# Convolution as three short filters over even and odd blocks, in place of four, in a two-layer convolution and feed-forward kernel

## The reference

```python
def _layer(x, style, w, b, mw, mb, typ):
    s = style @ mw.T + mb
    weight = SCALE * w * s[:, None, :, None]
    demod = lax.rsqrt(jnp.sum(weight * weight, axis=(2, 3)) + EPS)
    weight = weight * demod[:, :, None, None]
...
out = x
for i, typ in enumerate(('same', 'upsample', 'same', 'downsample')):
    out = _layer(out, style, weights[i], biases[i], mod_w[i], mod_b[i], typ)
```

## Time and profile before

| | |
|---|---|
| median of 3 runs | 1592.81 us (1592.79 to 1595.31) |
| the profiled execution, its own time | 1594.2 us |
| its span, first to last instruction | 1592.3 us |
| PE / PEld busy | 1559.0 / 1376.3 us |
| DVE / ACT / POOL busy | 798.6 / 577.3 / 206.4 us |
| mean granted clock of TensorE | 0.995 |
| one pair in the steady state, layer 0 / layer 1 | about 22.5 us / 23.5 us |

### The profile page before, as it was taken

How to read it: one execution, slowest core, us unless ns; L and a number is a source line. 1 busy time by engine, 2 the same in 40 slices (tenths; PEclk the granted TensorE clock), 3 DMA queues, 4 the chain that set the end, 5 groups by cost and what they waited for, 6 DMA issues and landing times.

```text
span 1592.3 us, 25445 instructions
## 1 busy us (share of the span) xinstructions
PE 1559.0 (98%) x8503; PEld 1376.3 (86%) x8503; DVE 798.6 (50%) x2061; ACT 577.3 (36%) x1291; POOL 206.4 (13%) x280
## 2 busy tenths in 40 slices
PE   5999999999999999999999999999999999999998
PEld 4688888888888888888868999999999999999998
DVE  7645655454444444454555554454555455445443
ACT  3323442334333333333333333333334333333332
POOL 1101010111011101111100110111111011011010
PEclk9999998999999999999999999999999999999999
DMA  4352332332333233333262333332332333333331
GB/s 103 99 117 82 106 80 64 95 101 83 102 83 105 81 104 79 105 92 92 66 185 67 79 96 88 79 105 79 83 101 79 99 85 89 96 79 99 86 79 66
DMA packets 54331, 145.66 MB, mean 91 GB/s; under 512 B 17233, under 2 KB 19345, under 8 KB 54306
## 3 DMA queue, kind: packets, MB, share of 16 engines
q1 hardware_dynamic: 53616, 144.96, 33.4%
q10 hardware_dynamic: 690, 0.37, 0.1%
HBM read 111.75 MB, written 33.55 MB: 91 GB/s over the span
## 4 chain that ended last, share of the span: by engine, by line
PE 93%; DVE 3%; issue 2%; DMA 1%; ACT 1%; POOL 0%; SPq 0%; DVEq 0%; POOLq 0%
PE bank L1099 29%; PE bank L1101 29%; PE bank L1100 28%; PE bank L1364 4%; PE bank L1246 1%; DMA xraw<-x_dram 1%; PE bank L1310 0%; PE bank L1281 0%; DVE fw_l L884 0%; DMA win<-in_L_cond_weights_dram 0%; PE bank L1176 0%; PE bank L1178 0%; PE bank L1300 0%; PE bank L1370 0%; DVE win L907 0%
## 5 line engine op out<-in xcount | busy, mean ns | idle before, releaser
L1099 PE MATMUL bank<-fw_h,ct_h 128*128 128x512 f32 (+2 forms) x1280 | 458.9, 358 | 0.6 <-DVE xout L856 0.5
L1100 PE MATMUL bank<-fw_l,ct_h 128*128 128x512 f32 (+2 forms) x1280 | 450.3, 352 | 0.0
L1101 PE MATMUL bank<-fw_h,ct_l 128*128 128x512 f32 (+2 forms) x1280 | 449.3, 351 | 0.0
L348 POOL TENSOR_TENSOR x_l<-xraw,x_h 128x512 fp32r<-128x512 f32 x128 | 165.8, 1317 | 1258.1 <-ACT x_h L488 1258.1
L992 DVE TENSOR_TENSOR ct_l<-bank,ct_h 128x384 fp32r<-128x384 f32 (+1 forms) x256 | 96.2, 417 | 390.3 <-ACT ct_h L536 389.8
L1101 PEld LDWEIGHTS bank<-fw_h,ct_l 128*128 128x128 f32 x1280 | 241.0, 188 | 22.7
L1099 PEld LDWEIGHTS bank<-fw_h,ct_h 128*128 128x128 f32 x1280 | 241.2, 188 | 20.8 <-issue 1.0
L1100 PEld LDWEIGHTS bank<-fw_l,ct_h 128*128 128x128 f32 x1280 | 241.6, 189 | 16.4
L1099 PE MATMUL bank<-x_h,tw 128*128 128x512 f32 x640 | 253.1, 395 | 0.5 <-DVE tw L977 0.5
L1101 PE MATMUL bank<-x_h,tw 128*128 128x512 f32 x640 | 252.8, 395 | 0.0
L1100 PE MATMUL bank<-x_l,tw 128*128 128x512 f32 x640 | 251.8, 394 | 0.0
(11 more groups left out here) (203 smaller groups left out, 1783.1 us busy)
## 6 DMA issues: line engine op xcount, KB each, us to landing
xraw<-in_x_dram SPq DMA_DIRECT2D x32, 512.0 KB, 5.0
xres<-in_x_dram SPq DMA_DIRECT2D x32, 512.0 KB, 3.9
x_dram<-xout SPq DMA_DIRECT2D x32, 512.0 KB, 2.9
xraw<-x_dram SPq DMA_DIRECT2D x32, 512.0 KB, 5.0
xres<-x_dram SPq DMA_DIRECT2D x32, 512.0 KB, 3.9
out_dram<-xout SPq DMA_DIRECT2D x32, 512.0 KB, 2.9
xraw<-in_x_dram SPq DMA_DIRECT2D x32, 511.5 KB, 6.5
xraw<-x_dram SPq DMA_DIRECT2D x32, 511.5 KB, 6.5
```

The costliest lines, as they stand in the source:

```text
L348: nc.gpsimd.tensor_tensor(x_l[h][:, PAD:PAD + HL], src, x_h[h][:, PAD:PAD + HL].bitcast(F32), ALU.subtract).then_inc(s["x_ready"], 1)
L1099: mm(out, wh, xh, start=start, stop=False, skip_group_check=True)
L1100: mm(out, wh, xl, start=False, stop=False, skip_group_check=True)
L1101: return mm(out, wl, xh, start=False, stop=stop, skip_group_check=True)
```

## The change

With the filter taps t0 to t4 and the columns of the image split into even and odd blocks, the change computes one product P of the odd columns with sums of neighbouring taps (three filter blocks), and two products of differences of neighbouring columns with the taps: even taps t0, t2, t4 (three blocks) and odd taps t1, t3 (two blocks). The even outputs are P plus the first, the odd outputs P minus the second. That is 8 filter blocks of 256 columns per image where 5 of 512 stood.

- POOL makes the differences (`neighbours`), two operations of 128x512 per pair, and takes the low parts of differences and odd columns (four operations). It starts on the input of pair j+1 only after `t_ready` and `t_side` of both images of pair j (`x_next`).
- ACT rounds odd columns and differences of pair j+1 after the convolution of pair j (`x_high`), copies the whole filter tile of 8 blocks (`t_high`) and takes over the copy across partitions of the second kind (`t_side`, two operations per image). It scales P (`sum_scaled`, 254 columns) where it scaled the whole result.
- DVE scales the 5 blocks into `t_f`, adds neighbours into 3 more, subtracts the high part (8 blocks), and copies 8 blocks across partitions; after each convolution it makes odd and even outputs (`conv_out`, two operations of 254 columns). `w2_low` and `prep` now come between `conv_out(j, 0)` and `conv_out(j, 1)`.
- P goes to `comp_ps[h]`, the two others to the halves of `conv_ps[h]`.

```diff
...
+                def neighbours(j):
+
+                    pool.wait_ge(s["x_load"], 32 * j + 32)
+                    for h in range(2):
+                        m0, m1 = (xraw[:, h, at:at + L].rearrange("p (n e q) -> p e n q", e=2, q=2)[:, :, :, 0] for at in (0, 2))
+                        nc.gpsimd.tensor_tensor(d_f[h][:, :, :], m0, m1, ALU.subtract).then_inc(s["d_made"], 1)
+
+                def split_low(j):
+                    for h in range(2):
+                        pool.wait_ge(s["x_hi"], 2 * j + h + 1)
+                        nc.gpsimd.tensor_tensor(d_l[h][:, :, 1:QL + 1], d_f[h][:, :, :], d_h[h][:, :, 1:QL + 1].bitcast(F32),
+                                                ALU.subtract)
+                        nc.gpsimd.tensor_tensor(o_l[h][:, 1:QL + 1], xraw[:, h, 2:L:4], o_h[h][:, 1:QL + 1].bitcast(F32),
+                                                ALU.subtract).then_inc(s["x_ready"], 1)
...
+                def x_next(j):
+
+                    pool.wait_ge(s["t_ready"], 2 * j + 2)
+                    pool.wait_ge(s["t_side"], 2 * j + 2)
+                    neighbours(j + 1)
+                    split_low(j + 1)
+
+                def body(j, last=False):
+
+                    pool.wait_ge(s["t_ready"], 2 * j + 2)
+                    edges(j)
+                    if not last:
+                        x_next(j)
...
+                def x_high(j, h, first=False):
+
                     if not first:
-                        act.wait_ge(s["conv_acc"], 2 * j)
-                    for h in range(2):
-                        nc.scalar.copy(x_h[h][:, PAD:PAD + HL],
-                                       xraw[:, h, :].rearrange("p (m q) -> p m q", q=2)[:, :, 0]).then_inc(s["x_hi"], 1)
+                        act.wait_ge(s["conv_acc"], 2 * j + h - 1)
+                    act.wait_ge(s["d_made"], 2 * j + h + 1)
+                    nc.scalar.copy(o_h[h][:, 1:QL + 1], xraw[:, h, 2:L:4])
+                    nc.scalar.copy(d_h[h][:, :, 1:QL + 1], d_f[h][:, :, :]).then_inc(s["x_hi"], 1)
...
                 def t_high(j):
                     for h in range(2):
-                        act.wait_ge(s["t_acc"], 2 * j + h + 1)
-                        nc.scalar.activation(tw[h][:, 0, :, 0, :], comp_ps[h][:, 0:NSH * C].rearrange("p (u c) -> p u c", c=C),
-                                             ACT.Copy, scale=s_all[:, 0, bass.ds(2 * j + h, 1)]).then_inc(s["t_hi"], 1)
+                        act.wait_ge(s["g_made"], 4 * j + 2 * h + 2)
+                        nc.scalar.copy(tw[h][:, 0, :, 0, :], t_f[h][:, :, :]).then_inc(s["t_hi"], 1)
+                    for h in range(2):
+
+                        act.wait_ge(s["t_lo"], 2 * j + h + 1)
+                        nc.scalar.copy(tw[h][half(0), :, 1:NSH, 1, :], tw[h][half(1), :, 0:NSH - 1, 0, :].bitcast(F32))
+                        nc.scalar.copy(tw[h][half(0), :, G0:SLOTS:G1 - G0, 1, :],
+                                       tw[h][half(1), :, 0:GM + 1:GM, 0, :].bitcast(F32)).then_inc(s["t_side"], 1)
...
-                def conv_scaled(j, h):
-                    act.wait_ge(s["conv_acc"], 2 * j + h + 1)
-                    nc.scalar.activation(conv[h][:, 2:HL - 2], conv_ps[h][:, 2:HL - 2], ACT.Identity,
+                def sum_scaled(j, h):
+
+                    act.wait_ge(s["p_acc"], 2 * j + h + 1)
+                    nc.scalar.activation(conv[h][:, 2:HL - 2:2], comp_ps[h][:, 1:QL - 1], ACT.Identity,
                                          scale=lam4[:, bass.ds(2 * j + h, 1)],
...
-                    conv_scaled(j, 0)
+                    sum_scaled(j, 0)
+                    if not composed:
+                        w2_high(ly, j + 1)
+                    if not last:
+                        x_high(j + 1, 0)
                     if step is not None:
                         prep(step)
-                    conv_scaled(j, 1)
+                    sum_scaled(j, 1)
+                    if not last:
+                        x_high(j + 1, 1)
...
                 def t_low(j):
                     for h in range(2):
+
+                        full = t_f[h]
+                        dve.wait_ge(s["t_acc"], 2 * j + h + 1)
+                        v.tensor_scalar(full[:, 0:NSH, :], comp_ps[h][:, 0:NSH * C].rearrange("p (u c) -> p u c", c=C),
+                                        s_all[:, 0, bass.ds(2 * j + h, 1)], None, ALU.mult).then_inc(s["g_made"], 1)
+                        dve.wait_ge(s["g_made"], 4 * j + 2 * h + 1)
+                        v.tensor_tensor(full[:, G0:SLOTS, :], full[:, 0:3, :], full[:, 1:4, :], ALU.add).then_inc(s["g_made"], 1)
+                    for h in range(2):
                         dve.wait_ge(s["t_hi"], 2 * j + h + 1)
-                        low(tw[h][:, 1, :, 0, :], comp_ps[h][:, 0:NSH * C].rearrange("p (u c) -> p u c", c=C),
-                            s_all[:, 0, bass.ds(2 * j + h, 1)], tw[h][:, 0, :, 0, :]).then_inc(s["t_lo"], 1)
+                        v.tensor_tensor(tw[h][:, 1, :, 0, :], t_f[h][:, :, :], tw[h][:, 0, :, 0, :].bitcast(F32),
+                                        ALU.subtract).then_inc(s["t_lo"], 1)
 
                         dve.wait_ge(s["t_lo"], 2 * j + h + 1)
-                        v.tensor_copy(tw[h][half(1), :, :, 1, :], tw[h][half(0), :, :, 0, :].bitcast(F32))
-                        v.tensor_copy(tw[h][half(0), :, 1:NSH, 1, :], tw[h][half(1), :, 0:NSH - 1, 0, :].bitcast(F32)
-                                      ).then_inc(s["t_ready"], 1)
+                        v.tensor_copy(tw[h][half(1), :, :, 1, :], tw[h][half(0), :, :, 0, :].bitcast(F32)).then_inc(s["t_ready"], 1)
...
+                def conv_out(j, h):
+
+                    dve.wait_ge(s["p_scaled"], 2 * j + h + 1)
+                    dve.wait_ge(s["conv_acc"], 2 * j + h + 1)
+                    even = conv[h][:, 2:HL - 2:2]
+                    stt(out=conv[h][:, 3:HL - 1:2], in0=conv_ps[h][:, QL + 1:2 * QL - 1], scalar=neg4[:, bass.ds(2 * j + h, 1)],
+                        in1=even, op0=ALU.mult, op1=ALU.add)
+                    stt(out=even, in0=conv_ps[h][:, 1:QL - 1], scalar=lam4[:, bass.ds(2 * j + h, 1)],
+                        in1=even, op0=ALU.mult, op1=ALU.add).then_inc(s["c_mid"], 1)
...
                     if not composed:
-                        compose_low(j, ly["lora"])
-                    elif ly["lora"]:
+                        compose_low(j)
+                    if ly["lora"]:
                         gates(j - 1)
+                    conv_out(j, 0)
+                    if not composed:
+                        w2_low(ly, j + 1)
                     if step is not None:
                         prep(step)
+                    conv_out(j, 1)
                     turned_low(j, 0)
...
                 def stage_conv(j, h, first=False):
+
                     pe.wait_ge(s["t_ready"], 2 * j + h + 1)
+                    pe.wait_ge(s["t_side"], 2 * j + h + 1)
                     pe.wait_ge(s["x_ready"], 2 * j + h + 1)
+                    for i, slot in enumerate((G0, G1, 4)):
+                        last = conv_tap(h, comp_ps[h][:, 0:QL], slot, o_h[h][:, i:i + QL], o_l[h][:, i:i + QL], i == 0, i == 2)
+                    last.then_inc(s["p_acc"], 1)
                     if not first:
                         pe.wait_ge(s["ct_ready"], 4 * j)
-                    for u in range(NSH):
-                        last = three(conv_ps[h][:, :], flat(tw[h][:, 0, u, :, :]), flat(tw[h][:, 1, u, :, :]),
-                                     x_h[h][:, u:u + HL], x_l[h][:, u:u + HL], u == 0, u == NSH - 1)
+                    for i, slot in enumerate((0, 2, 4)):
+                        conv_tap(h, conv_ps[h][:, 0:QL], slot, d_h[h][:, 0, i:i + QL], d_l[h][:, 0, i:i + QL], i == 0, i == 2)
+                    for i, slot in enumerate((1, 3)):
+                        last = conv_tap(h, conv_ps[h][:, QL:2 * QL], slot, d_h[h][:, 1, i:i + QL], d_l[h][:, 1, i:i + QL], False, i == 1)
                     last.then_inc(s["conv_acc"], 1)
...
```

150 lines of the change are left out of this document (77 added, 73 removed).

## The result

| | before | after |
|---|---|---|
| median of the runs | 1592.8 us | 1618.42 us (1616.13 to 1620.65) |
| span of the profiled execution | 1592.3 us | 1614.3 us |
| that execution's own time | 1594.2 us | 1616.13 us |
| PE's share of the chain that ended last | 93% | 81% |

The account below looks back on a forecast made before the run. PE was taken as the bound, holding 93% of the chain that ended last. 1592.3 - 81 + 43.8 + 16.5 + 39.7 + 8 = 1619.3 us, with the median 0.5 above the span: 1620 us, range 1565 to 1680.

Parts of the forecast that it names:

- the one I held likeliest: Whole kernel: PE's saving is there but its waits outweigh it, 1606 to 1640 us; chance 0.38.
- 1. PE's saving: PE's convolution: 48 matmuls of 256 columns replace 30 of 512, 1.265 us per pair, 81 us gained.
- 2. filter later: Head of stage_conv: PE waits for the filter 0.55 us (layer 0) and 0.91 (layer 1) per pair, 43.8 us lost.
- 3. holding in layer 1: Turn of layer 1: POOL holds off DVE's operations, conv_out(1) comes late, PE waits 0.55 us per pair, 16.5 us lost.
- 4. preparation pairs: Layer 0, pairs 2 to 8 and 31: DVE's preparation starts only after conv_out(0) and w2_low, 39.7 us lost.
- 5. starts of the layers: Layer starts: POOL's differences ahead of ACT, longer DVE chain of the feed-forward split; 8 us lost, between 3 and 12.
- Rival D: Head of stage_conv: the filter is in time, the 43.8 us loss goes, 1576 us; chance 0.22.
- rival A: DVE's small gate operations in layer 1 are held too, PE waits 2.0 to 3.2 us, 1680 us; chance 0.17.
- signs that I named: Changed profile: among others, stage_turn waiting for conv_buf in layer 1; gates over 4 us long would point to rival A.
- Rival C: Steady state: no holding, DVE's operations slip between POOL's, 16.5 and 12 us go, 1591 us; chance 0.17.
- rival E: Preparation pairs: PE's waits bring its clock down, some 2 us each in eight pairs, 1636 us; chance 0.03.

Follow-up runs that it names:

- e2: Changed kernel with PE's order of layer 1 alone altered, two more feed-forward chunks between stage_t and the convolution: 1601.5 us, ratio 1.0054.
- e11: Changed kernel with POOL's differences cut to one column in the loop, except each layer's first and last pair: 1617.1 us, ratio 1.0143.
- e4: Changed kernel with SP's loads of the input alone moved earlier: 1609.1 us, ratio 1.0096.
- e9: Kernel before the change with the earlier loads of the input alone: 1592.4 us, ratio 0.9994.

## Why the prediction was right

The forecast, 1620 us, is 0.1% from the measured 1618.4. The case that happened is the one I held likeliest: the saving is there, and PE's waits for the filter and the preparation eat more than all of it. That the number is so near is luck. Its terms, taken from the ledger and the readings above (the measured values of 4 and 5 are what the ledger leaves there beside the savings and waits of 1 and 2):

| step | forecast | measured |
|---|---|---|
| 1. PE's saving | -81 | -72.6 |
| 2. filter later | +43.8 | +30.6 |
| 3. holding in layer 1 | +16.5 | 0 |
| 4. preparation pairs | +39.7 | +42.9 |
| 5. starts of the layers | +8 | +20.9 |
| sum | +27.0 | +21.8 |

The terms are off by +8.4, -13.2, -16.5, +3.2 and +12.9 us, which add up to -5.2. The span is 1614.3 us where 1619.3 was forecast, and the median comes out right because it lies 4.1 us above that span and not 0.5.

1. **Saving.** 1.12 and 1.15 us a pair in place of 1.265: 48 matmuls take 0.1213 us each, not 0.1186. The third starts 0.31 us behind the first (506.08 to 506.39), where 0.24 is the pace further on, and I had taken the pace from inside a short series. That is 0.07 of the 0.13 us; the rest is a pace of 0.120 to 0.121 in place of 0.1186.
2. **Filter.** Its pieces are within 0.01 us of the forecast (0.55, 0.36, 0.62, 0.68, 0.62, 0.40). PE starts at t0+3.50 where I had 3.63, and the 0.09 for refilling the pipeline belongs to step 1. 0.33 x 30 and 0.69 x 30 is 30.6. Steps 1 and 2 together: -42.0, forecast -37.2. Rival D, the filter in time, fell: e2 shows its price in layer 1, 0.64 us a pair.
3. **Holding.** The term that was mis-sized most: 0.55 us a pair forecast, nothing measured (e11). The mechanism is there, and wider than forecast, since the small operations are held too. This is rival A: the Trainium skill (SBUF — State Buffer, "SBUF: two separate sides") says that whoever starts first has the shared pair for its whole instruction, and the trace agrees with 0.56 us for 0.23 and 1.06 for 0.18. The step that failed is the end of the two w2_low. I had each held by a low part of POOL, to T+7.2; they end at T+6.7 (1247.25 less 1240.58), and conv_out(1) at T+7.45 where I had T+8.1. The turn comes at T+7.4 and wants image 1 some 0.35 later, T+7.7 where I had T+7.55. So 0.55 us too late became 0.3 us early. A's price of 2.0 to 3.2 us fell by the same slack, and because the last operation of the gates slipped in ahead of POOL's next. Of the signs that I named, the wait at layer 1's turn is the one that is absent; the gates take 3.5 us (1241.68 to 1245.15), under the 4 that I had set for A. Rival C had the right price for the plain pairs, nothing, but for a reason that layer 1 refutes: it had DVE's operations slip between POOL's.
4. **Preparation.** Right in size, by two errors that cancel. PE's waits there are 21.5 + 3.6 + 2.7 + 2.2, and 1.1 in pair 31: 31.1 us. The forecast had 39.7 of waiting, because it started the steps at T+6.2 behind a held w2_low; they start at T+4.5 (152.75 against 148.21) behind a w2_low that isn't held, and are themselves stretched (step 3 takes 9.4 us where it took 6.2). The remaining 11.8 us are not waits that the profile lists. They are PE's slower pace behind the waits, as far as the clock's windows show it: the estimate from them is 11 us. This is rival E, which I gave 0.03 as a case by itself where it was a part of every case in which PE waits long for the preparation.
5. **Starts.** Undersized, 8 for 20.9 (16.4 in the ledger and 1.13 for each of four pairs). I said of SP's load that it "is issued an iteration earlier than needed". That holds in the loop, not at pair 2, where it stands behind the residual's and the parameters' loads; e4 gets 5.8 and 4.2 us of it back, and e9 shows that the kernel before did not need it. The other 11 us are near the 8 forecast; how they divide among the longer filter, the conv_outs and the clock was not tested.

## What to carry to other kernels

When a change takes work from the bound engine and gives it to its helpers, price the regular stretch and the irregular ones (starts of layers, steps inserted in some iterations) apart: here the regular pairs gained 31 us and the irregular ones lost 53. A burst of work on a helper costs what exceeds its longest gap, and can be had for less by cutting it: here 24 of 43 us came back. Before a stretched operation is given a price, look for the next thing that its engine waits for.
